# Attention with a mixture-of-experts layer: head pairs as two 64-row tiles of the PE array, two-bank maxima, two PSUM rings, and an instruction order written by a greedy planner

## What is computed

```python
mod = (silu(c) @ wmod)              # sa, ca, ga, sb, cb, gb: six vectors of 128
h = layernorm(x) * (1 + ca) + sa
q, k, v = h @ Wq, h @ Wk, h @ Wv    # 16 heads of 8 columns, rotary on q and k
scores = q @ k.T / sqrt(8)          # per head 2048 x 2048, causal
x = x + ga * (softmax(scores) @ v) @ Wo
h = layernorm(x) * (1 + cb) + sb
# 8 experts, top 2 by h @ w_g, capacity 640 tokens each, in rank order
x = x + gb * sum_k p_k * (gelu(h @ c_fc[e_k]) @ c_proj[e_k])
```

## Time and profile before

| what | value |
|---|---|
| median of 3 runs | 691.77 us (690.76 to 692.2) |
| span of the profiled execution | 684.6 us |
| median less span (launch and end) | 7.2 us |
| TensorE busy | 564.4 us, 82% of the span |
| VectorE busy | 449.5 us, 66% |
| ScalarE busy | 350.3 us, 51% |
| GpSimd busy | 207.4 us, 30% |
| mean granted TensorE clock | 0.931 |
| chain that ended last | PE 59%, DVE 21%, DMA 6% |

### The profile page before, as it was taken

The page is one execution under the profiler, slowest core; times in us unless marked ns, Lnnn a source line. Parts: engine busy times, 40 slices in busy tenths (PEclk is TensorE's granted clock), DMA queues, the critical chain, the costliest instruction groups (busy, mean ns, idle before and its releaser), DMA issues.

```text
span 684.6 us, 10732 instructions
## 1 busy us (share of the span) xinstructions
PE 564.4 (82%) x3592; PEld 249.6 (36%) x3592; DVE 449.5 (66%) x1004; ACT 350.3 (51%) x736; POOL 207.4 (30%) x501
## 2 busy tenths in 40 slices
PE   3164878899998999989999999899988841999980
PEld 2042433344332333333333334233321131687770
DVE  3866889698899898989898988898700061112123
ACT  1200424567666765747677767577788710223220
POOL 6203424512314823025202013034020224055461
PEclk9676999999999999999999999999999975799995
DMA  8830805541140611100000000000000002022206
GB/s 192 224 52 3 179 11 139 142 128 38 45 125 13 193 36 44 30 20 29 5 1 3 1 2 1 1 17 17 1 3 1 0 1 70 1 71 64 65 35 192
DMA packets 43523, 37.63 MB, mean 55 GB/s; under 512 B 4880, under 2 KB 39097, under 8 KB 43436
## 3 DMA queue, kind: packets, MB, share of 16 engines
q1 hardware_dynamic: 39312, 30.64, 17.2%
q0 software_dynamic: 2448, 4.63, 1.9%
q10 hardware_dynamic: 1708, 1.67, 1.2%
HBM read 20.39 MB, written 17.05 MB: 55 GB/s over the span
## 4 chain that ended last, share of the span: by engine, by line
PE 59%; DVE 21%; DMA 6%; issue 4%; POOL 4%; ACT 3%; SPq 3%; POOLq 0%; ACTq 0%; DVEq 0%
PE av L1163 17%; PE score L1147 14%; DVE mpart L877 12%; PE work L1125 11%; PE work L1255 6%; PE av L1269 4%; ACT PRB L714 3%; PE work L1128 1%; PE work L1099 1%; SPq L423 1%; DMA k_rows<-part 1%; DMA m_rows<-mrow 1%; PE score L1269 1%; PE work L1188 1%; POOL slots_x L647 1%
## 5 line engine op out<-in xcount | busy, mean ns | idle before, releaser
L714 ACT ACTIVATE PRB<-score 128x512 f32<-128x512 f32 (+3 forms) x640 | 300.8, 540 | 161.8 <-PE score L1147 159.1
L877 DVE TENSOR_REDUCE mpart<-work 128x1 f32<-128x512 f32 (+3 forms) x560 | 339.5, 668 | 58.1 <-PE work L1125 35.0
L1125 PE MATMUL work<-KS,QP 128*128 128x512 bf16 (+3 forms) x640 | 213.0, 356 | 39.0 <-DMA QP<-q_rows 19.2
L1147 PE MATMUL score<-QP,KS 128*128 128x512 bf16 (+3 forms) x640 | 213.5, 353 | 17.4 <-DMA QP<-m_rows 8.1
L1163 PE MATMUL av<-PRB,VX 128*9 128x512 f32 (+3 forms) x1264 | 144.8, 540 | 0.0
L610 POOL TENSOR_SCALAR_AFFINE_SELECT PRB<-PRB 128x128 f32<-128x128 f32 x256 | 70.6, 294 | 176.9 <-ACT PRB L714 174.0
L1147 PEld LDWEIGHTS score<-QP,KS 128*128 128x128 bf16 x640 | 59.1, 98 | 178.1 <-ACT PRB L714 112.3
L1125 PEld LDWEIGHTS work<-KS,QP 128*128 128x128 bf16 x640 | 64.0, 100 | 93.4 <-DVE mpart L877 42.8
L756 ACT ACTIVATE QP<-work 128x640 f32<-128x640 f32 x32 | 22.5, 703 | 72.5 <-PE work L1255 72.5
L660 POOL DMA_INDIRECT parts_y<-KS,back_to x40 | 38.9, 971 | 55.0 <-DVEq L1051 45.0
L1128 PE MATMUL work<-causal,identb 128*128 128x128 bf16 x256 | 51.8, 229 | 0.0
(11 more groups left out here) (163 smaller groups left out, 359.5 us busy)
## 6 DMA issues: line engine op xcount, KB each, us to landing
q_rows<-part SPq DMA_DIRECT2D x24, 128.0 KB, 2.3
KS<-k_rows SPq DMA_DIRECT2D x16, 192.0 KB, 4.7
k_rows<-part SPq DMA_DIRECT2D x21, 128.0 KB, 2.3
slots_x<-RT SPq DMA_DIRECT2D x8, 325.0 KB, 3.6
KS<-slots_x SPq DMA_DIRECT2D x8, 325.0 KB, 3.1
W<-in_L_ffn_c_proj_dram SPq DMA_DIRECT2D x4, 512.0 KB, 5.4
CS<-in_L_ffn_c_fc_dram SPq DMA_DIRECT2D x4, 512.0 KB, 5.5
PRB<-parts_y SPq DMA_DIRECT2D x8, 256.0 KB, 4.2
```

The source lines that it names most:

```text
L714: a.activation(PRB[:, t % PR, q0:QB], SC[t % 3][:, q0:QB], ACT.Exp, scale=SCALE).then_inc(exped, 1)
L877: v.tensor_reduce(mpart[:, u % 2, cols, k0 // QB], w[:, 0:len(heads) * keys].rearrange("p (j k) -> p j k", k=keys), AX.X, ALU.max).then_in ...
L1125: last = t_.matmul(row, QP[:, h % 2, h // 2, b % 2, (i % TB) * P:(i % TB + 1) * P], KS[:, h // 2, k0:k0 + keys], start=True, stop=not ends)
L1147: t_.matmul(SC[t % 3][:, q0:QB], KS[:, h // 2, kt * P:(kt + 1) * P], QP[:, h % 2, h // 2, b % 2, q0:QB], start=True, stop=True).then_inc(s ...
```

## The change

**Pairs.** `QP` loses its zero rows: one 128-row operand holds both heads of a pair, one in partitions 0 to 63, the other in 64 to 127. The two heads are two matmuls of 48 rows (51 in the score pass), each on its own half of the array's rows and into its own bank. The mask is now two matmuls of 64 rows for each half, as 64 rows can't hold a 128-row identity; four DMAs at the start make the swapped halves of `mask_i` and `mask_c`.

**Maxima over two banks.** A piece is a pair (two pairs where 2 x keys <= 512), VectorE reduces both banks in one instruction. There are 288 pieces where there were 560 reductions. `q` and `qr` (and `k`, `kr`) become one step with two banks.

**Rings.** VectorE's steps use `DW` = 2 slots of two banks each, ScalarE's steps (`xt`, `v`, `negmax`, `ot`, `h2t`, `score`) share the `AW` = 3 banks. A score step takes two of the three banks, so it waits for the exp of two tiles before its first.

**Order.** `Planner` keeps a model clock for PE, DVE and ACT and appends whichever step could start first by its costs. Block 1's projections stand ahead of all maxima. SyncE now follows the plan, with `expand(b)` at `("k", b)`.

```diff
-NW = 4
+DW = 2
+AW = 3
 PR = 16
+D_KIND = ("mod", "q", "k", "max", "norm", "wo", "logit", "rank", "tail")
+A_KIND = ("xt", "v", "negmax", "ot", "h2t", "score")
...
-        pieces += [((j,), i, k0, QB) for k0 in range(0, QB * b, QB) for j in range(GH)]
+        pieces += [((a,), i, k0, QB) for k0 in range(0, QB * b, QB) for a in range(GH // 2)]
         keys = P * (i + 1) - QB * b
-        n = QB // keys
-        pieces += [(tuple(range(j, min(j + n, GH))), i, QB * b, keys) for j in range(0, GH, n)]
+        if 2 * keys <= QB:
+            pieces.append(((0, 1), i, QB * b, keys))
+        else:
+            pieces += [((a,), i, QB * b, keys) for a in range(GH // 2)]
...
+LAUNCH_AT = {2: 3, 3: 5}
+class Planner:
+    def __init__(self):
+        self.plan = [("ln", 0), ("xt", 0), ("mod", 0), ("q", 0), ("k", 0), ("ln", 1), ("mod", 1)] + projections(1)[:4]
+        self.plan += [("v", 0), ("v", 1)]
...
+        self.d_step(("max", u, n), at, len(pairs) * (keys / 2200 + 0.03 + 0.13 * masked), 0.13 + 2 * len(pairs) * keys / 960)
...
+        self.pe = at + wide / 2200 + 0.04
+        for half in range(2):
+            self.a_bank(0.18 + wide / 1200)
...
+                choices.append((self.d_start(), (-1 if lead < LEAD else 2) if self.dve - self.pe < 1.0 else 4, "max", None))
...
+                    choices.append((waiting, 0 if self.act - self.pe < 0.8 else 3, "score", None))
...
+                    choices.append((at, 3.5, "av", None))
+            at, _, what, chain = min(choices, key=lambda c: (c[0], c[1]))
...
+LEAD = 1.5
...
-        QP = sb("QP", [P, 2, NPAIR, 2, QB], bf16)
+        QP = sb("QP", [P, NPAIR, 2, QB], bf16)
...
+            for s in plan:
+                if s[0] == "k":
+                    expand(s[1])
+                    if s[1] == 0:
+                        swap_masks()
+                elif s[0] == "negmax":
+                    put_negmax(s[1])
+                    if ("k", NB - 1) in plan[:plan.index(s)] or went < E:
+                        for load, n in loads[went:went + 4]:
+                            load(n)
+                        went += 4
...
+                    if len(pairs) == 1:
+                        v.tensor_reduce(part[:, :, pairs[0], i % TB], w[:, :, 0:keys], AX.X,
+                                        ALU.max).then_inc(slot_free(s), 1)
...
+            def take_bank(step, n=0):
+                r = aring[step] + n
+                if r >= AW:
+                    wait_bank(pe, r - AW)
+                return SC[r % AW], a_full[r % AW]
...
+                    for n, a in enumerate(pairs):
+                        done = n == len(pairs) - 1
+                        for half in range(2):
+                            rows = slice(64 * half, 64 * half + ROWS)
+                            last = t_.matmul(w[:, half, n * keys:(n + 1) * keys],
+                                             QP[rows, 2 * g + a, b % 2, (i % TB) * P:(i % TB + 1) * P],
+                                             KS[rows, 2 * g + a, k0:k0 + keys], start=True, stop=not ends)
...
+                    banks = [take_bank(s, half) for half in range(2)]
+                    for half, (w, ok) in enumerate(banks):
+                        rows = slice(64 * half, 64 * half + KROWS)
+                        t_.matmul(w[:, q0:QB], KS[rows, 2 * g + a, kt * P:(kt + 1) * P],
+                                  QP[rows, 2 * g + a, b % 2, q0:QB], start=True, stop=True).then_inc(ok, 1)
```

More of the change, by code:

```diff
@@ L196, in __init__ @@
-        self.diag = {}
-        for s in self.plan:
-            if s[0] == "score" and s[2] >= TB * units()[s[1]][0]:
-                self.diag[s[1:]] = len(self.diag) + 1
+            if s[0] not in A_KIND:
+                continue
+            self.aring[s] = len(self.bank_use)
+            if s[0] != "score":
+                self.areads[s] = len(self.areads) + 1
+                self.bank_use.append(("read", self.areads[s]))
+                continue
+            _, u, kt, a = s
+            for half in range(2):
+                j = 2 * a + half
+                self.tile[u, kt, j] = len(self.tile)
+                self.bank_use.append(("exp", len(self.tile)))
+                if kt >= TB * units()[u][0]:
+                    self.diag[u, kt, j] = len(self.diag) + 1
@@ L475, in _, with swap_masks @@
             loads += [(load_w1, n) for n in range(E // 2)] + [(fill_parts, n) for n in range(TOPK * NT // CT + 1)]
[L476 to L483 removed]
+            def swap_masks():
+                sp.wait_ge(const_ok, 2)
+                for half in range(2):
+                    other = slice(64 * (1 - half), 64 * (1 - half) + 64)
+                    for mask in (mask_i, mask_c):
+                        sp.dma_start(mask[64 * half:64 * half + 64, 1, :], mask[other, 0, :]).then_inc(mask_in, 16)
+            went = 0
+            for s in plan:
[9 more added lines that the diff above has]
+                        went += 4
+                elif s[0] == "score":
+                    _, u, kt, a = s
+                    b = units()[u][0]
+                    if u % NG == NG - 1 and kt == TB * (b + 1) - 1 and a == GH // 2 - 1 and b + 2 < NB:
+                        reload_q(b + 2, st.tile[u, kt, GH - 1])
+            assert went >= len(loads)
             sp.wait_ge(scattered, 16 * TOPK * NT)
@@ L1075, in _ @@
                     w, ok = take(s)
+                    w = w[:, 0, :]
                     pe.wait_ge(silu_ok, 1)
@@ L1121, in _ @@
                     ends = k0 + keys == P * (i + 1)
-                    for n, j in enumerate(heads):
-                        h = GH * g + j
-                        row = w[:, n * keys:(n + 1) * keys]
-                        last = t_.matmul(row, QP[:, h % 2, h // 2, b % 2, (i % TB) * P:(i % TB + 1) * P],
-                                         KS[:, h // 2, k0:k0 + keys], start=True, stop=not ends)
-                        if ends:
-                            last = t_.matmul(row[:, keys - P:keys], identb[:, :], causal[:, :],
-                                             start=False, stop=True)
```

526 lines of the change are left out of this document (292 added, 234 removed).

## The result

| | kernel before | changed kernel |
|---|---|---|
| median | 691.26 us (689.61 to 692.2, 4 runs) | 748.31 us (745.11 to 764.42, 4 runs) |
| ratio | | 1.081, 95% interval 1.0777 to 1.0843 |
| span of the profiled execution | 684.6 us | 762.7 us |
| mean granted clock | 0.931 | 0.779 |
| end of attention (last copy out of `AV`) | 547 | 623 |

The forecast was 651 us, 40 less; it became 57 more. (The profiled execution of the changed kernel took 764.42 us, 16 more than the median, at a clock some 0.03 under that of the others, so I use it for lengths and waits and the medians for time; its block lengths and low clocks are a little worse than usual.)

A forecast was written before the change was run, and what follows sets the result against it. TensorE was taken to set the pace, VectorE close behind. First scores at 73.2 plus blocks of 48.5, 92, 128 and 165 end attention at 507, not 547; span 644.6 plus 7.2 gave 651 (640 to 664; with rivals 630 to 690).

The forecast's parts named there:

- The pair: On TensorE, two heads' matmuls on disjoint row halves stream together: 0.25 us a pair, bounds 0.215 and 0.43.
- Rival 1: On TensorE, a pair's halves run one after the other, 0.43 us a pair: about +13, 705 us; chance 12%.
- Rival 2: On TensorE, weight loads of the same half are not hidden, 0.35 us a pair: 671 us; chance 15%.
- Rival 4: The two rings keep VectorE full, at 97% from 73 on: attention ends at 490, total 635 us; chance 10%.
- The key tile: One key tile of four heads with maxima, at full clock, takes 2.67 us, against 2.81 before.
- Two-bank maxima: On VectorE, one maximum over two banks costs 1.14 us; all maxima together take 19 us less.
- The start: First scores start at 73.2 us instead of 66.85, with unit 1's rows following at once.
- The tail: The last 138 us, after attention, stay: the same matmuls, and the experts' second buffer only moves.
- the ring of the scores: The next score pair issues when this one's first exp ends: 1.14 us a pair, if TensorE is free then.
- the block sums: Blocks 0 to 3 after the first scores take 48.5, 92, 128 and 165 us; attention ends at 507.
- the 7.2 us of launch and end: Added to the forecast span of 644.6 us; median less span of the kernel before, taken as unchanged.
- Rival 3: TensorE's clock falls because it streams less, at half clock a key tile some 3.5 us: 661 to 684; chance 15%.

The follow-up runs named there:

- experiment 13: Kernel before, with VectorE's ring of four banks handed out in twos: 701.61 us, ratio 1.026.
- experiment 12: Changed kernel, each half waiting for its own bank, with a unit's last two `av` and copy moved behind three score pairs of the next unit: 711.19 us, ratio 1.034.
- Experiment 4: Kernel before, order and rings unchanged, with a single head's matmuls reading 48 or 51 rows instead of 128: 712.66 us, ratio 1.035.
- halves apart: Changed kernel, with each half of a score pair waiting only for its own bank: 720.87 us, ratio 1.050 to the kernel before.
- experiment 8: Kernel before, with two scores one behind the other, the first waiting for both banks: 711.77 us, ratio 1.035.
- experiment 11: Changed kernel with the old order, full-height matmuls, each half waiting for its own bank, and no wait for the copied mask: 733.47 us, ratio 1.067.
- experiment 10: Changed kernel's order and rings with full-height matmuls and each half waiting for its own bank: 718.69 us, ratio 1.041.
- experiment 5: Changed kernel's order and rings, with score and maximum matmuls over all 128 rows: 739.35 us, ratio 1.077 to the kernel before.
- experiment 7: Changed kernel's rings and two-bank maxima, with the order of the kernel before and full-height matmuls: 766.13 us, ratio 1.116.
- experiment 1: Changed kernel with every pair's matmuls of both passes issued twice: 791.75 us, ratio 1.144 to the kernel before.

## Why the prediction was wrong

**Right.** The pair: 0.22 to the next one (taken 0.25). Rivals 1, 2 and 4 are false: nothing runs serially, same-half loads are hidden, and VectorE is at 77% at most. The Trainium skill's rule that a load overlaps a running matmul only when the row groups differ ("TensorE: Matmul & The Clock Gate", Part 3, Packing small matmuls) does not hold for these tiles either. The loads of 0.10 us for both halves stand at 521.39, beside the pair that started at 521.38, and the next pair of the same rows is 0.22 behind. The key tile at full clock: 2.75 (said 2.67). Two-bank maxima: 1.13 apart (said 1.14), 19 us off VectorE (said 19). The start: 73.0 (said 73.2), unit 1 right behind. The tail: 140 (said 138). The count of the engines' work was right nearly everywhere, and the time wrong by 97 us.

**The step that failed** is the ring of the scores: "The next pair is issued when the first exp of this one ends", "1.14 us a pair", "if TensorE is free at that moment", and the block sums made from it (92, 128 and 165 for blocks 1 to 3; 121, 161 and 207 in the profiled execution). I priced the ring as a cadence with TensorE free, added the `av` once, and so treated the wait for two of three banks as costless otherwise. It halves ScalarE's cover. The experiments price it four times: 24 us when the kernel before is given it, 21 to 27 when the changed kernel loses it, and 26 to 27 in blocks 1 to 3 at full height, in either order, where nothing but the wait changed there.

The quiet key tile was right (2.75), the unit was not. Unit 12 of the changed kernel, at full clock, takes 46.8 us where the sum had 41.3. From the last copy before it to its first `av` pass 6.7 us, and the next eleven steps to another `av` take 2.87 each on average, with the steps of the epilogue between them.

**Not priced at all:** VectorE's two slots. I only asked what a two-bank maximum costs, not that TensorE gets its next bank back in steps of two: 16 to 18 us on the kernel before (experiment 13). The 19 us of gain for VectorE came, and were lost in its waits. Nor did I price the greedy order against the old one: 18 us in blocks 1 to 3. Part of it is the ends of units: I counted "8 to 9" for the last four key tiles and nothing for the change of unit, but the order drains ScalarE there (21 to 25 us in the profiles, 10 won back by experiment 12). What block 0 took over its 48.5, 12 us, no experiment explains. And the 7.2 us of launch and end on top of the span were too many: in every run whose span and time are both recorded it is 1.5 to 1.9 (745.11 against 743.4 here), so the profiled execution before must have been some 5 us under its median, which is an estimate.

**Rival 3, the falling clock, came true beside the ring, but not for TensorE's idling alone.** I tied the clock to that idling and gave +10 to +33. Experiment 4 shows a lower clock at a busy share at which full-height kernels kept theirs: +3.5%, 22 to 24 us on the kernel before. What half-height tiles cost net is less where they run in pairs: 0.4% in the changed kernel (ratio 1.081 against 1.077 at full height), 0.9% with halves apart (1.050 against 1.041), 1.9% in the old order (1.135 against 1.116). At half clock a key tile with maxima is 4.23, not the 3.5 that I took, since the longer `av` stands in the ring of one exp's cover: clock and ring multiply. Unit 15, which has no maxima, shows it: 33.4 us before, 36.2 with the pair's wait at full clock (experiment 8), 48.4 in the changed kernel at 0.61.

Together, step by step at full height and nearly full clock, blocks 1 to 3 take 403 us before, 422 in the new rings with halves apart (experiment 11), 440 with the greedy order too (experiment 10) and 467 with the pair's wait too (experiment 5). That is 19 + 18 + 27 = 64 us, less 7 in block 0: 57 in the profiled executions, 53 by the medians. The half height adds 0.4% (3 us), and the changed kernel lost 57 by the medians. The parts that were put on the kernel before alone, 3.5% (pair wait), 2.6% (two slots) and 3.5% (half height) less 0.7% for the start, come to 8.9% without the greedy order, against 8.1% measured. The parts are not independent, so this says that the size is accounted for and not how much belongs to each.

What stays open: the last 26 us of experiment 12 over the kernel before. It still has the two slots and the half-height tiles; a version of it without either was not tried. Nor do these runs settle why half-height tiles lower the clock: half of the rows standing still and less of the time filled were not told apart.

## What to carry to other kernels

A ring of three that is handed out in twos gives its reader one item of cover, not two, and a two-bank slot does the same to a ring of four: before pairing work on an engine with slack, ask how long the longest other step in its queue is, and whether the reader's cover is longer (cover: the work that the reader still has while the feeder is held up). Here that step was 1.0 us and the cover 0.5. Halving TensorE's work was no gain where TensorE fed two engines through small rings, and part of the time saved came back as a lower clock. Price a ring at the moment the feeding engine is busy, at both levels of the clock; and let each half of a pair wait only for its own bank.

## What the runs showed of the hardware

- With matmuls that use 48 or 51 of 128 rows, 27% of which start together with the one before, the granted clock was 0.91 to 0.94 at a busy share of 89 to 93% (experiment 4); full-height kernels had 0.98 or more at 85 to 91% (experiments 7, 8 and 13). In the changed kernel it was 0.79 to 0.83, and 0.99 in block 2 when every pair was issued twice (experiment 1). At 0.61 (575 to 623 of the changed kernel) most of a stretch is at the level of 1.2 GHz.
- Two row tiles stream at the same time: two 512-column matmuls in the 0.22 us of one, with the next loads of the same halves (0.10 us) hidden.
- Maxima over two banks (1,024 columns) stand 1.13 us apart in a row, against 1.21 for two of one bank: 0.08 us is saved per instruction. One alone is 1.22 us long.
